# Moving steps between slots and engines in a split-fp32 macaron layer: the weights' transposes, the affinities, and five low parts of W_down

## The chip, the core and the metric

The kernel runs on one core of a Trainium2 chip. The metric is the device time of one execution, in microseconds. Its engines named here: TensorE (PE in the profile, with its weight loads as PEld), VectorE (DVE), ScalarE (ACT), GpSimd (POOL), SyncE (SP), which issues the transfers. Each works through its own instructions in the order in which they were written; semaphores hold an instruction until another engine's is done.

## What is computed

Eight sequences of 512 tokens and 128 features go through a feed-forward layer, an attention-like gate and the same feed-forward layer again.

```python
x = x + 0.5 * ffn(layernorm(x))
x = x + attn(layernorm(x))
x = x + 0.5 * ffn(layernorm(x))

# ffn, TOP_K = 8, 64 experts, each 128 -> 64 -> 128
shared = silu(xf @ Ws_up) @ Ws_down
aff = xf @ centroids.T
_, idx = top_k(aff + expert_biases, TOP_K)
w = sigmoid(take_along_axis(aff, idx, axis=1))
w = w / (sum(w) + 1e-8)
cw = zeros.at[tokens, idx].add(w)
h = silu(einsum('td,edf->etf', xf, W_up))
y = einsum('etf,efd->etd', h, W_down)
out = shared + einsum('etd,te->td', y, cw)

# attn: xf, xb are u times WB, WBf, with the first and the last row kept as they are
gamma = sigmoid(xf @ w1.T + xb @ w2.T + b)
y = gamma * (xf + xb) + (1 - gamma) * u
```

All experts are computed for all tokens; the routing enters as the weights cw, zero for an expert that was not chosen.

## The kernel before

**Phases and tiles.** One feed-forward layer of one sequence is a phase: 16 phases, numbered from 0. Even phases are a sequence's first layer, odd ones its second. Between the two lies the attention of that sequence, which is worked in the following phase beside other work. A phase has 33 tiles of 128 hidden features by 512 tokens: tile 0 is the shared expert, the others two features of each of the 64 experts. For each tile TensorE makes an up product into one of five PSUM banks (`up`), ScalarE applies silu, VectorE multiplies by `cw` (`gate`), ScalarE rounds to the high part `g_hi`, and VectorE (even tiles) or GpSimd (odd tiles) makes the low part `g_lo` by subtraction. A down product adds the tile into `y_ps`.

**Split products.** Each fp32 operand is split into a high and a low part, and a product is three matmuls, high by high, low by high, high by low (`split_product`, L697). The parts of W_up and W_down are made once, in phase 0, in eight pieces each: ScalarE makes the high parts (`wu_hi`, `wd_hi`), VectorE and GpSimd the low parts (`wu_lo`, `wd_lo`).

**Slots.** Every engine walks through a phase in 35 slots (`SLOTS`). In slot t TensorE does the down product of tile t-6 (`LAG`), then the up product of tile t. A down product waits for the low part of its tile (L755); an up product waits until the bank of tile t-5 is free, which for odd tiles is the gate's end and for even ones the low part's (`free_bank`, L766). Slots 0 to 5 still do down products of the phase before.

**Side steps.** What prepares the next phase or finishes the last is put between the tiles by tables, one for each kind of phase: a name and the slot after whose tile work the step stands. The same table is read by every engine. `AT_FIRST` is for phase 0, `AT_SECOND` for 1, `AT_THIRD` for 2, `AT_STEADY_A` and `AT_STEADY_B` for the loop's two phases (L119; it runs five times: phases 3 and 4, up to 11 and 12), and others for the last three. The steps that matter here, in their order:

- `x_t`, `x_hi`, `x_lo`: normalized tokens transposed by TensorE into `side1`, high part on ScalarE, low part on VectorE.
- `aff` (TensorE, L719, waits for x_lo), `aff_sum`, `bias`, `max`, `take` (VectorE), `sig` (ScalarE, which loads another activation table and then silu's again), `gate`, `sum`, `eps`, `inv` (VectorE), `cw` (GpSimd writes `w_dup`, L344), `cw_t` (TensorE transposes it into `side0`, L708), `cw_copy` (ScalarE, L404).
- `x1`, `stat1`, `aggr1`, `rstd1`, `norm1` (VectorE, with rstd on GpSimd), `xu` (GpSimd), `u_t` (TensorE, into `side1`), `u_copy` (ScalarE), `attn` (TensorE, L735, over both side banks, waits for u_copy and, in phases 2, 4, ..., 12, for cw_copy), `tanh` (ScalarE), `gamma` (GpSimd), `t1`, `x2` (VectorE), and again statistics and a normalization (`stat2` to `norm2`).

In phases 2, 4, ..., 12 all three chains run; in phase 0 the first two, and the splitting of the weights.

Of the kernel before, what the change touches and what calls it, by code (L numbers as in the profile page):

```python
# [17 lines left out]
LAG = RING + 1  # L18
# [18 lines left out]
class Phase:  # L37
# [19 lines left out]

NORM0 = ("stat0", "aggr0", "rstd0", "norm0")
AT_FIRST = {
    "x_t": 11, "x_hi": 12, "x_lo": 13, "aff": 15, "aff_sum": 15, "sig": 17, "bias": 16, "max": 17, "take": 17,  # L60
    "gate": 19, "sum": 21, "eps": 22, "inv": 24, "cw": 25, "cw_t": 33, "cw_copy": 33,
    "stat0": (1, 2), "aggr0": 3, "rstd0": 3, "norm0": (5, 6),
    "v": 11, "v_copy": 14, "wu_hi": (None, None, 2, 5, 8, 12, 15, 20),
    "wu_lo": (None, None, 3, 6, 9, 11, 17, 21), "wd_hi": (None, 4, 6, 12, 14, 19, 22, 26),
    "wd_lo": (None, 4, 8, 13, 16, 20, 24, 28),
    "late": 3,
}
AT_SECOND = {
# [6 lines left out]
    "y": 2, "keep": 26,  # L75
}
AT_THIRD = {
    "x_t": 4, "x_hi": 5, "x_lo": 5, "aff": 7, "aff_sum": 7, "sig": 9, "bias": 8, "max": 9, "take": 9,
    "gate": 11, "sum": 14, "eps": 15, "inv": 17, "cw": 18, "cw_t": 21, "cw_copy": 21,
    "y_t": 6, "x1": 8, "stat1": (10, 12), "aggr1": 13, "rstd1": 14, "norm1": (16, 18), "xu": 19, "u_t": 22,  # L80
    "u_copy": 22, "attn": 25, "tanh": 25, "gamma": 25, "t1": 25, "x2": (27, 28),
    "stat2": (29, 30), "aggr2": 30, "rstd2": 31, "norm2": (33, 34),
    "late": 3,
}
AT_STEADY_A = {
# [5 lines left out]
}  # L91
AT_STEADY_B = {
    "x_t": 1, "x_hi": 2, "x_lo": 4, "aff": 7, "aff_sum": 7, "sig": 9, "bias": 8, "max": 9, "take": 9,
    "gate": 11, "sum": 14, "eps": 15, "inv": 17, "cw": 18, "cw_t": 21, "cw_copy": 21,
    "y_t": 6, "x1": 8, "stat1": (10, 12), "aggr1": 13, "rstd1": 14, "norm1": (16, 18), "xu": 19, "u_t": 22,
    "u_copy": 22, "attn": 25, "tanh": 25, "gamma": 25, "t1": 25, "x2": (27, 28),
    "stat2": (29, 30), "aggr2": 30, "rstd2": 31, "norm2": (33, 34),
    "y": 2,
}
AT_MID_PREP = {  # L100
# [28 lines left out]
def build(nc, x, ident_in, cent_t, ebias, ws_up, ws_down, w_up, w_down, wb, wb_t, wbf, wbf_t, w1, w2, b_in, out):  # L129
    fp32, fp32r = mybir.dt.float32, mybir.dt.float32r  # L130
    ALU, ACT, AX = mybir.AluOpType, mybir.ActivationFunctionType, mybir.AxisListType
    ctx = ExitStack()
    with ctx:
        def sb(name, shape, dt=fp32):
            return ctx.enter_context(nc.sbuf_tensor(name, shape, dt))

        def sem(name):
            return ctx.enter_context(nc.semaphore(name))


# [39 lines left out]
        th, gamma = sb("th", [P, NB]), sb("gamma", [P, NB])  # L180
# [5 lines left out]
        aff = sb("aff", [P, NB, E])  # L186
        sig, biased, taken = sb("sig", [P, NB, E]), sb("biased", [P, NB, E]), sb("taken", [P, NB, E])
# [15 lines left out]
        consts_set, v_done, sm_hi_done, sm_lo_done = (sem(s) for s in ("consts_set", "v_done", "sm_hi_done", "sm_lo_done"))  # L203
        ce_hi_done, ce_lo_done = sem("ce_hi_done"), sem("ce_lo_done")
        v_copied, half_b_done = sem("v_copied"), sem("half_b_done")
        wu_hi_done, wd_hi_done, wd_lo_done = sem("wu_hi_done"), sem("wd_hi_done"), sem("wd_lo_done")
        wu_lo_done = [sem("wu_lo_done_vector"), sem("wu_lo_done_pool")]
        up_done, silu_done, gate_done, hi_done = (sem(s) for s in ("up_done", "silu_done", "gate_done", "hi_done"))
        lo_done = [sem("lo_done_vector"), sem("lo_done_pool")]
# [123 lines left out]
        @block.gpsimd  # L333
        def _(pool):
            def rstd_of(k, c):

                hold(pool, mv_done[k], c + 1)
                nc.gpsimd.tensor_scalar_add(var_eps[k][:, :], mv[k][:, :, 1], LN_EPS).then_inc(eps_done[k], 1)
                pool.wait_ge(eps_done[k], c + 1)
                nc.gpsimd.tensor_tensor(rstd[k][:, :], var_eps[k][:, :], neg_half[:, :], ALU.pow).then_inc(rstd_done[k], 1)  # L340

            def spread(q, n):
                pool.wait_ge(inv_done[q], n + 1)
                nc.gpsimd.tensor_tensor(*spread_operands, ALU.mult).then_inc(dup_done[q], 1)  # L344

            def low_part(ph, t):

                i = t % GRING
                pool.wait_ge(hi_done, NT * ph.p + t + 1)
                nc.gpsimd.tensor_tensor(g_lo[:, i, :], gated[:, t // 2 % ORING, :], g_hi[:, i, :].bitcast(fp32),  # L350
                                        ALU.subtract).then_inc(lo_done[1], 1)

            def split_up(i):

                js = slice(i * JS, (i + 1) * JS)
                pool.wait_ge(wu_hi_done, i + 1)
                nc.gpsimd.tensor_tensor(wu_lo[:, js, :], wu_raw[:, js, :], wu_hi[:, js, :].bitcast(fp32),
                                        ALU.subtract).then_inc(wu_lo_done[1], 1)

            def phase(ph):  # L360
                for t in range(SLOTS):
                    if (t - 1) % 2 and 0 < t <= NT:
                        low_part(ph, t - 1)
                    if t in ph.at.get("wu_lo", ()):
                        split_up(ph.at["wu_lo"].index(t))
                    for k, c in ((0, ph.norm0), (1, ph.mid), (2, ph.mid)):
                        if ph.at.get(f"rstd{k}") == t:
                            rstd_of(k, c)
                    if ph.at.get("xu") == t:
                        pool.wait_ge(norm_done[1], ph.mid + 1)  # L370
                        nc.gpsimd.tensor_tensor(xu[:, :, :], x1[:, :, :], normed[1][:, :, :], ALU.add).then_inc(xu_done, 1)
                    if ph.at.get("gamma") == t:

                        hold(pool, tanh_done, ph.mid + 1)
                        nc.gpsimd.tensor_scalar(gamma[:, :], th[:, :], 0.5, 0.5, ALU.mult, ALU.add).then_inc(gamma_done, 1)
                    if ph.at.get("keep") == t:

                        if ph.post is not None:
                            pool.wait_ge(out_done, ph.post + 1)
                        hold(pool, x2_done, ph.keep + 1)  # L380
# [12 lines left out]
        def _(act):
# [100 lines left out]
        def _(dve):  # L494
# [99 lines left out]
            def phase(ph):  # L594
                q = 1 - ph.q
                n = ph.prep[0] if ph.prep else None
                for t in range(SLOTS):
# [94 lines left out]
        def _(pe):  # L692
# [183 lines left out]
```

## Time and profile before

| | us |
|---|---|
| median of 3 runs | 828.2 (828.01 to 828.98) |
| profiled execution | 827.39 |
| its span | 825.6 |
| TensorE matmuls busy | 804.7 (97%) |
| VectorE busy | 690.8 (84%) |
| ScalarE busy | 653.8 (79%) |
| GpSimd busy | 402.9 (49%) |

The span is from the first to the last instruction of the profiled execution. Busy times of matmuls overlap: one 128x512 matmul is listed with about 0.40 us and the next starts 0.23 us after it. A row of a timeline gives start, duration, engine, source line, operation, output and inputs, and in brackets the idle time ahead of it with what ended it. Line numbers are those of the kernel before.

### The profile page before, as it was taken

How to read it: one execution, taken by the hardware profiler on the slowest of the kernel's cores; microseconds unless marked ns; L12 is line 12 of the kernel's file. 1: busy time of each engine (PE TensorE's matmuls, PEld its weight loads, DVE VectorE, ACT ScalarE, POOL GpSimd, SP SyncE). 2: the span in 40 equal slices, each digit the busy share in tenths (PEclk: the TensorE clock that was granted, in tenths of full speed). 3: DMA queues.
4: the chain of work that ended last, by engine and by line, in shares of the span. 5: the costliest groups of instructions: out<-in, count | busy, mean ns of one | idle time of the engine just before them, and what ended most of it. 6: DMA issues, size and time to landing. Idle time of an engine off the chain costs nothing.

```text
span 825.6 us, 12468 instructions
## 1 busy us (share of the span) xinstructions
PE 804.7 (97%) x3691; PEld 650.5 (79%) x3691; DVE 690.8 (84%) x1456; ACT 653.8 (79%) x1204; POOL 402.9 (49%) x355
## 2 busy tenths in 40 slices
PE   7899999999999999999999999999999999999998
PEld 5677877788887888878887888878888788888786
DVE  7898988888898887988879788797897978788875
ACT  5888678778797787877978778886888878876975
POOL 2654543545455454555535445353463644554443
PEclk9999999999999999999999999999999999999999
DMA  7000000000000000000000000000000000000000
GB/s 267 20 0 13 14 1 1 0 1 27 13 0 1 13 13 13 0 0 25 0 13 0 0 25 0 13 0 0 25 0 0 0 1 27 0 1 1 14 0 14
DMA packets 16046, 11.51 MB, mean 14 GB/s; under 512 B 1680, under 2 KB 14992, under 8 KB 16016
## 3 DMA queue, kind: packets, MB, share of 16 engines
q1 hardware_dynamic: 16016, 11.15, 4.3%
q8 instruction: 15, 0.25, 0.1%
q14 instruction: 15, 0.12, 0.1%
HBM read 9.05 MB, written 2.10 MB: 13 GB/s over the span
## 4 chain that ended last, share of the span: by engine, by line
PE 71%; DVE 16%; ACT 7%; issue 3%; POOL 3%; DMA 0%; DVEq 0%; ACTq 0%; POOLq 0%
PE up L700 11%; PE up L701 11%; PE up L699 11%; PE y_ps L699 11%; PE y_ps L701 10%; PE y_ps L700 10%; DVE up L568 3%; DVE gated L568 3%; PE side L708 3%; ACT g_hi L417 3%; DVE g_lo L577 2%; DVE normed L514 2%; ACT up L409 2%; POOL g_lo L350 1%; ACT L409 1%
## 5 line engine op out<-in xcount | busy, mean ns | idle before, releaser
L350 POOL TENSOR_TENSOR g_lo<-gated,g_hi 128x512 fp32r<-128x512 f32 x256 | 331.8, 1296 | 371.5 <-ACT g_hi L417 371.5
L409 ACT ACTIVATE up<-up 128x512 f32<-128x512 f32 x528 | 310.6, 589 | 82.1 <-PE up L701 80.0
L568 DVE TENSOR_TENSOR gated<-up,cw 128x512 f32<-128x512 f32 x256 | 175.2, 684 | 57.3 <-ACT up L409 53.3
L699 PE MATMUL y_ps<-g_hi,wd_hi 128*128 128x512 f32 x512 | 208.3, 407 | 1.8 <-POOL g_lo L350 1.7
L699 PE MATMUL up<-x_hi,wu_hi 128*128 128x512 f32 x512 | 202.6, 396 | 1.9 <-DVE g_lo L577 1.8
L701 PE MATMUL y_ps<-g_hi,wd_lo 128*128 128x512 f32 x512 | 202.6, 396 | 0.0
L700 PE MATMUL up<-x_lo,wu_hi 128*128 128x512 f32 x512 | 202.5, 396 | 0.0
L701 PE MATMUL up<-x_hi,wu_lo 128*128 128x512 f32 x512 | 201.7, 394 | 0.0
L700 PE MATMUL y_ps<-g_lo,wd_hi 128*128 128x512 f32 x512 | 201.5, 394 | 0.0
L568 DVE TENSOR_TENSOR up<-up,cw 128x512 f32<-128x512 f32 x256 | 176.3, 689 | 24.4 <-ACT up L409 21.4
L417 ACT CAST g_hi<-up 128x512 fp32r<-128x512 f32 x272 | 160.8, 591 | 36.8 <-DVE up L568 34.5
L577 DVE TENSOR_TENSOR g_lo<-up,g_hi 128x512 fp32r<-128x512 f32 x256 | 174.3, 681 | 10.6 <-ACT g_hi L417 9.3
L417 ACT CAST g_hi<-gated 128x512 fp32r<-128x512 f32 x256 | 157.3, 615 | 30.8 <-DVE gated L568 28.6
L699 PEld LDWEIGHTS up<-x_hi,wu_hi 128*128 128x128 f32 x512 | 96.3, 188 | 26.3 <-DVE g_lo L577 2.2
L699 PEld LDWEIGHTS y_ps<-g_hi,wd_hi 128*128 128x128 f32 x512 | 96.4, 188 | 25.4 <-POOL g_lo L350 3.7
L701 PEld LDWEIGHTS y_ps<-g_hi,wd_lo 128*128 128x128 f32 x512 | 96.2, 188 | 23.1
L700 PEld LDWEIGHTS up<-x_lo,wu_hi 128*128 128x128 f32 x512 | 96.3, 188 | 23.0
L701 PEld LDWEIGHTS up<-x_hi,wu_lo 128*128 128x128 f32 x512 | 96.3, 188 | 22.5
L700 PEld LDWEIGHTS y_ps<-g_lo,wd_hi 128*128 128x128 f32 x512 | 96.5, 189 | 18.8
L514 DVE TENSOR_SCALAR normed<-x,mv,rstd 128x128 f32<-128x128 f32 x64 | 35.1, 599 | 0.9 <-POOL rstd L340 0.9
L577 DVE TENSOR_TENSOR g_hi<-up,g_hi 64x512 fp32r<-64x512 f32 x16 | 11.1, 695 | 23.2 <-ACT g_hi L417 23.2
L340 POOL TENSOR_TENSOR rstd<-var_eps,neg_half 128x4 f32<-128x4 f32 x24 | 25.3, 1053 | 2.0
(100 smaller groups left out, 564.2 us busy)
## 6 DMA issues: line engine op xcount, KB each, us to landing
x_in<-in_x SPq DMA_DIRECT2D x8, 256.0 KB, 2.7
wu_raw<-in_w_up SPq DMA_DIRECT2D x4, 512.0 KB, 6.0
wd_raw<-in_w_down SPq DMA_DIRECT2D x4, 512.0 KB, 7.0
x_res<-in_x SPq DMA_DIRECT2D x8, 256.0 KB, 2.8
out<-out_sb SPq DMA_DIRECT2D x7, 256.0 KB, 2.2
out<-out_sb SPq DMA_DIRECT2D x2, 128.0 KB, 1.8
sm_raw<-in_ident SPq DMA_DIRECT2D x2, 64.0 KB, 5.4
ident<-in_ident SPq DMA_DIRECT2D x1, 64.0 KB, 2.3
```

The source lines that it names most:

```text
L340: nc.gpsimd.tensor_tensor(rstd[k][:, :], var_eps[k][:, :], neg_half[:, :], ALU.pow).then_inc(rstd_done[k], 1)
L350: nc.gpsimd.tensor_tensor(g_lo[:, i, :], gated[:, t // 2 % ORING, :], g_hi[:, i, :].bitcast(fp32), ALU.subtract).then_inc(lo_done[1], 1)
L409: nc.scalar.activation(up[i][:, :], up[i][:, :], ACT.Silu).then_inc(silu_done, 1)
L417: nc.scalar.copy(g_hi[:, t % GRING, :], src).then_inc(hi_done, 1)
L514: made = nc.vector.tensor_scalar(normed[k][:, n, :], norm_from[k][:, n, :], mv[k][:, n, 0:1], rstd[k][:, n:n + 1], ALU.subtract, ALU.mult)
L568: nc.vector.tensor_tensor(gated[:, t // 2 % ORING, :] if t % 2 else up[i][:, :], up[i][:, :], cw[ph.q][:, :], ALU.mult).then_inc(gate_done, 1)
L577: nc.vector.tensor_tensor(lo[ps, i, :], up[t % RING][ps, :], g_hi[ps, i, :].bitcast(fp32), ALU.subtract).then_inc(lo_done[0], 1)
L699: nc.tensor.matmul(o, a[0], b[0], start=start, stop=False)
L700: nc.tensor.matmul(o, a[0], b[1], start=False, stop=False)
L701: return nc.tensor.matmul(o, a[1], b[0], start=False, stop=stop)
L708: last = nc.tensor.transpose(rows(dst, n), src(n), ident[:, :])
```

## The change

It moves entries of three tables and gives part of one step to another engine.

- In `AT_THIRD` and `AT_STEADY_B` (phases 2, 4, ..., 12) `cw_t` and `cw_copy` go from slot 21 to 23, `attn`, `tanh`, `gamma`, `t1` from 25 to 26, `x2`, `stat2`, `aggr2`, `rstd2` one slot back.
- In `AT_THIRD` (phase 2 only) `aff` and `aff_sum` go from 7 to 9, `bias`, `sig`, `max`, `take`, `gate` two slots back, `sum` and `eps` one.
- In `AT_FIRST` (phase 0) `x_lo` goes from 13 to 12, `aff` and what follows it up to `eps` one slot back.
- Of the eight pieces of `wd_lo`, VectorE makes the first three as before, GpSimd the other five, in slots 13, 15, 20, 23 and 27 (they were in 13, 16, 20, 24 and 28 on VectorE). TensorE waits for GpSimd's pieces on a semaphore of their own.

```diff
+VW = 3
@@ AT_FIRST
-    "x_t": 11, "x_hi": 12, "x_lo": 13, "aff": 15, "aff_sum": 15, "sig": 17, "bias": 16, "max": 17, "take": 17,
-    "gate": 19, "sum": 21, "eps": 22, "inv": 24, "cw": 25, "cw_t": 33, "cw_copy": 33,
+    "x_t": 11, "x_hi": 12, "x_lo": 12, "aff": 16, "aff_sum": 16, "sig": 18, "bias": 17, "max": 18, "take": 18,
+    "gate": 20, "sum": 22, "eps": 23, "inv": 24, "cw": 25, "cw_t": 33, "cw_copy": 33,
...
-    "wd_lo": (None, 4, 8, 13, 16, 20, 24, 28),
+    "wd_lo": (None, 4, 8, 13, 15, 20, 23, 27),
@@ AT_THIRD
-    "x_t": 4, "x_hi": 5, "x_lo": 5, "aff": 7, "aff_sum": 7, "sig": 9, "bias": 8, "max": 9, "take": 9,
-    "gate": 11, "sum": 14, "eps": 15, "inv": 17, "cw": 18, "cw_t": 21, "cw_copy": 21,
+    "x_t": 4, "x_hi": 5, "x_lo": 5, "aff": 9, "aff_sum": 9, "sig": 11, "bias": 10, "max": 11, "take": 11,
+    "gate": 13, "sum": 15, "eps": 16, "inv": 17, "cw": 18, "cw_t": 23, "cw_copy": 23,
...
-    "u_copy": 22, "attn": 25, "tanh": 25, "gamma": 25, "t1": 25, "x2": (27, 28),
-    "stat2": (29, 30), "aggr2": 30, "rstd2": 31, "norm2": (33, 34),
+    "u_copy": 22, "attn": 26, "tanh": 26, "gamma": 26, "t1": 26, "x2": (28, 29),
+    "stat2": (30, 31), "aggr2": 31, "rstd2": 32, "norm2": (33, 34),
@@ AT_STEADY_B: cw_t, cw_copy, attn to rstd2 as in AT_THIRD
...
@@ GpSimd
+            def split_down(i):
+                js = slice(i * JS, (i + 1) * JS)
+                pool.wait_ge(wd_hi_done, i + 1)
+                nc.gpsimd.tensor_tensor(wd_lo[:, js, :], wd_raw[:, js, :], wd_hi[:, js, :].bitcast(fp32),
+                                        ALU.subtract).then_inc(wd_lo_done[1], 1)
...
                     if t in ph.at.get("wu_lo", ()):
                         split_up(ph.at["wu_lo"].index(t))
+                    if t in ph.at.get("wd_lo", ())[VW:]:
+                        split_down(ph.at["wd_lo"].index(t))
@@ VectorE
-                    if t in ph.at.get("wd_lo", ()):
+                    if t in ph.at.get("wd_lo", ())[:VW]:
@@ TensorE
-                        pe.wait_ge(wd_lo_done, (t - LAG - 1) // JS + 1)
+                        i = (t - LAG - 1) // JS
+                        pe.wait_ge(wd_lo_done[i >= VW], i + 1 - VW * (i >= VW))
```

TensorE's queue in phase 2 around slots 21 and 22, before. `w_dup` are the spread weights, `normed1` the tokens for the attention; a product is three rows:

```order
L701 MATMUL up1<-x_hi0,wu_lo 128x512
L708 MATMUL side<-ident,w_dup 128x128 x4
L699 MATMUL y_ps<-g_hi,wd_hi 128x512
L700 MATMUL y_ps<-g_lo,wd_hi 128x512
L701 MATMUL y_ps<-g_hi,wd_lo 128x512
L699 MATMUL up2<-x_hi0,wu_hi 128x512
L700 MATMUL up2<-x_lo0,wu_hi 128x512
L701 MATMUL up2<-x_hi0,wu_lo 128x512
L708 MATMUL side<-ident,normed1 128x128 x4
L699 MATMUL y_ps<-g_hi,wd_hi 128x512
```

The same place after the change, slots 22 and 23. The line numbers are those of the changed file:

```order
L713 MATMUL up2<-x_hi0,wu_lo 128x512
L720 MATMUL side<-ident,normed1 128x128 x4
L711 MATMUL y_ps<-g_hi,wd_hi 128x512
L712 MATMUL y_ps<-g_lo,wd_hi 128x512
L713 MATMUL y_ps<-g_hi,wd_lo 128x512
L711 MATMUL up3<-x_hi0,wu_hi 128x512
L712 MATMUL up3<-x_lo0,wu_hi 128x512
L713 MATMUL up3<-x_hi0,wu_lo 128x512
L720 MATMUL side<-ident,w_dup 128x128 x4
L711 MATMUL y_ps<-g_hi,wd_hi 128x512
```

The weights' transposes stood ahead of the u transposes, at the end of slot 21; they now stand behind them, at the end of slot 23, two down and two up products later. Phases 4 to 12 have the same order.

GpSimd's queue in phase 0 from slot 11, before. `g_lo` are low parts of odd tiles, `wu_lo` and `wd_lo` pieces of the weights' low parts:

```order
L357 TENSOR_TENSOR wu_lo<-wu_raw,wu_hi 128x512
L350 TENSOR_TENSOR g_lo<-gated,g_hi 128x512 x3
L357 TENSOR_TENSOR wu_lo<-wu_raw,wu_hi 128x512
L350 TENSOR_TENSOR g_lo<-gated,g_hi 128x512 x2
L357 TENSOR_TENSOR wu_lo<-wu_raw,wu_hi 128x512
L350 TENSOR_TENSOR g_lo<-gated,g_hi 128x512 x2
L344 TENSOR_TENSOR w_dup<-w_sel,w_inv 128x512
L350 TENSOR_TENSOR g_lo<-gated,g_hi 128x512 x8
```

And after the change:

```order
L360 TENSOR_TENSOR wu_lo<-wu_raw,wu_hi 128x512
L353 TENSOR_TENSOR g_lo<-gated,g_hi 128x512
L367 TENSOR_TENSOR wd_lo<-wd_raw,wd_hi 128x512
L353 TENSOR_TENSOR g_lo<-gated,g_hi 128x512
L367 TENSOR_TENSOR wd_lo<-wd_raw,wd_hi 128x512
L353 TENSOR_TENSOR g_lo<-gated,g_hi 128x512
L360 TENSOR_TENSOR wu_lo<-wu_raw,wu_hi 128x512
L353 TENSOR_TENSOR g_lo<-gated,g_hi 128x512 x2
L367 TENSOR_TENSOR wd_lo<-wd_raw,wd_hi 128x512
L360 TENSOR_TENSOR wu_lo<-wu_raw,wu_hi 128x512
L353 TENSOR_TENSOR g_lo<-gated,g_hi 128x512
L367 TENSOR_TENSOR wd_lo<-wd_raw,wd_hi 128x512
```

Five pieces of `wd_lo` have come between the low parts (the fifth stands four rows further on). Around slots 20 to 22 two pieces stand between the low parts of tiles 19 and 21.

VectorE's queue in phase 0 from slot 12, before. `gated<-up3` is the gate of tile 13, `up2<-up2` that of tile 12:

```order
L568 TENSOR_TENSOR up2<-up2,cw0 128x512
L568 TENSOR_TENSOR gated<-up3,cw0 128x512
L577 TENSOR_TENSOR g_lo<-up2,g_hi 128x512
L583 TENSOR_TENSOR wd_lo<-wd_raw,wd_hi 128x512
L521 TENSOR_TENSOR x_lo1<-side,x_hi1 128x512
L568 TENSOR_TENSOR up4<-up4,cw0 128x512
L609 TENSOR_SCALAR b_half<-b_col 128x1
L611 COPY sm_raw<-side 128x2
L612 COPY sm_raw<-side 128x2
L568 TENSOR_TENSOR gated<-up0,cw0 128x512
```

And after the change:

```order
L580 TENSOR_TENSOR up2<-up2,cw0 128x512
L533 TENSOR_TENSOR x_lo1<-side,x_hi1 128x512
L580 TENSOR_TENSOR gated<-up3,cw0 128x512
L589 TENSOR_TENSOR g_lo<-up2,g_hi 128x512
L580 TENSOR_TENSOR up4<-up4,cw0 128x512
L621 TENSOR_SCALAR b_half<-b_col 128x1
L623 COPY sm_raw<-side 128x2
L624 COPY sm_raw<-side 128x2
L580 TENSOR_TENSOR gated<-up0,cw0 128x512
L589 TENSOR_TENSOR g_lo<-up4,g_hi 128x512
```

`x_lo1`, for which the affinities wait, has gone ahead of tile 13's gate and low part, and `wd_lo` is gone from between.

## Rows read from the trace of the kernel before

**Rows 1.** Page, busy us of each engine, share of the span, instructions.

```profile
PE 804.7 (97%) x3691; PEld 650.5 (79%) x3691; DVE 690.8 (84%) x1456; ACT 653.8 (79%) x1204; POOL 402.9 (49%) x355
```

**Rows 2.** Waits of TensorE: us in total, times, longest.

```profile
PE side L708 <- POOL w_dup L344: 5.9, 7, 0.9
PE side L719 <- DVE x_lo L521: 4.1, 3, 2.6
...
PE up L699 <- DVE g_lo L577: 1.8, 3, 0.9
```

**Rows 3.** TensorE timeline, phase 4, slots 21 to 23; last row 100 us on (start, us, instruction, [idle]).

```profile
251.24 0.39 PE L701 MATMUL up<-x_hi,wu_lo 128*128 128x512 f32 x1
252.55 0.66 PE L708 MATMUL side<-ident,w_dup 128*128 128x128 f32 x4 [0.92 <-POOL w_dup L344]
252.96 0.48 PE L699 MATMUL y_ps<-g_hi,wd_hi 128*128 128x512 f32 x1
...
253.75 0.39 PE L699 MATMUL up<-x_hi,wu_hi 128*128 128x512 f32 x1
...
254.45 0.60 PE L708 MATMUL side<-ident,normed 128*128 128x128 f32 x4
254.80 0.47 PE L699 MATMUL y_ps<-g_hi,wd_hi 128*128 128x512 f32 x1
...
255.58 0.39 PE L699 MATMUL up<-x_hi,wu_hi 128*128 128x512 f32 x1
...
352.44 0.66 PE L708 MATMUL side<-ident,w_dup 128*128 128x128 f32 x4 [0.86 <-POOL w_dup L344]
```

**Rows 4.** VectorE timeline, phase 4: second half of the normalization, low part of tile 18.

```profile
250.66 1.92 DVE L514 TENSOR_SCALAR normed<-x,mv,rstd 128x128 f32<-128x128 f32 x2
...
253.10 0.67 DVE L577 TENSOR_TENSOR g_lo<-up,g_hi 128x512 fp32r<-128x512 f32 x1
```

**Rows 5.** GpSimd timeline, phase 4: spread weights.

```profile
251.46 1.04 POOL L344 TENSOR_TENSOR w_dup<-w_sel,w_inv 128x512 f32<-128x512 f32 x1
```

**Rows 6.** ScalarE timeline, phase 4: high part in slot 23.

```profile
257.49 0.63 ACT L417 CAST g_hi<-up 128x512 fp32r<-128x512 f32 x1
```

**Rows 7.** TensorE timeline, phase 4: start of attention.

```profile
259.07 0.38 PE L740 MATMUL side<-sm_raw,u_mid 128*128 128x130 f32 x2
```

**Rows 8.** TensorE timeline, phase 2: last up matmul of slot 7, affinities, next product.

```profile
129.72 0.40 PE L701 MATMUL up<-x_hi,wu_lo 128*128 128x512 f32 x1
...
131.07 0.33 PE L719 MATMUL side<-ce_both,x_hi 128*128 128x128 f32 x1 [0.96 <-DVE x_lo L521]
...
131.99 0.48 PE L699 MATMUL y_ps<-g_hi,wd_hi 128*128 128x512 f32 x1
```

**Rows 9.** VectorE timeline, phase 2: second half of the normalization.

```profile
150.77 1.92 DVE L514 TENSOR_SCALAR normed<-x,mv,rstd 128x128 f32<-128x128 f32 x2
```

**Rows 10.** TensorE timeline, phase 0: slot 15, affinities, down product 21, phase 1's start.

```profile
35.09 0.40 PE L701 MATMUL up<-x_hi,wu_lo 128*128 128x512 f32 x1
38.05 0.33 PE L719 MATMUL side<-ce_both,x_hi 128*128 128x128 f32 x1 [2.55 <-DVE x_lo L521]
...
55.91 0.39 PE L699 MATMUL y_ps<-g_hi,wd_hi 128*128 128x512 f32 x1
...
67.47 0.39 PE L699 MATMUL up<-x_hi,sm_hi 128*128 128x512 f32 x1
```

**Rows 11.** VectorE's wd_lo from 30 to 66 us: duration ns min/median/max.

```profile
L583 DVE TENSOR_TENSOR wd_lo<-wd_raw,wd_hi x6: 680/1539/1810, 28.6 to 62.4; 128x512 fp32r<-128x512 f32 x6
```

**Rows 12.** VectorE timeline, phase 0: gate of tile 13 and the idle time before it.

```profile
35.51 0.69 DVE L568 TENSOR_TENSOR gated<-up,cw 128x512 f32<-128x512 f32 x1 [1.73 <-ACT up L409]
```

**Rows 13.** GpSimd, groups from 36 to 66 us: busy, mean ns, idle before.

```profile
L350 POOL TENSOR_TENSOR g_lo<-gated,g_hi 128x512 fp32r<-128x512 f32 x10 | 13.1, 1306 | 13.1 <-ACT g_hi L417 13.1
L357 POOL TENSOR_TENSOR wu_lo<-wu_raw,wu_hi 128x512 fp32r<-128x512 f32 x2 | 3.5, 1736 | 0.0
```

**Rows 14.** GpSimd timeline, phase 0: low part of tile 19.

```profile
50.55 1.30 POOL L350 TENSOR_TENSOR g_lo<-gated,g_hi 128x512 fp32r<-128x512 f32 x1 [1.91 <-ACT g_hi L417]
```

More of the change, by code:

```diff
@@ L93 @@
     "x_t": 1, "x_hi": 2, "x_lo": 4, "aff": 7, "aff_sum": 7, "sig": 9, "bias": 8, "max": 9, "take": 9,
-    "gate": 11, "sum": 14, "eps": 15, "inv": 17, "cw": 18, "cw_t": 21, "cw_copy": 21,
+    "gate": 11, "sum": 14, "eps": 15, "inv": 17, "cw": 18, "cw_t": 23, "cw_copy": 23,
     "y_t": 6, "x1": 8, "stat1": (10, 12), "aggr1": 13, "rstd1": 14, "norm1": (16, 18), "xu": 19, "u_t": 22,
-    "u_copy": 22, "attn": 25, "tanh": 25, "gamma": 25, "t1": 25, "x2": (27, 28),
-    "stat2": (29, 30), "aggr2": 30, "rstd2": 31, "norm2": (33, 34),
+    "u_copy": 22, "attn": 26, "tanh": 26, "gamma": 26, "t1": 26, "x2": (28, 29),
+    "stat2": (30, 31), "aggr2": 31, "rstd2": 32, "norm2": (33, 34),
     "y": 2,
@@ L205, in build @@
         v_copied, half_b_done = sem("v_copied"), sem("half_b_done")
-        wu_hi_done, wd_hi_done, wd_lo_done = sem("wu_hi_done"), sem("wd_hi_done"), sem("wd_lo_done")
+        wu_hi_done, wd_hi_done = sem("wu_hi_done"), sem("wd_hi_done")
+        wd_lo_done = [sem("wd_lo_done_vector"), sem("wd_lo_done_pool")]
         wu_lo_done = [sem("wu_lo_done_vector"), sem("wu_lo_done_pool")]
@@ L604, in phase @@
                         low_part(ph, t - 1)
-                    if t in ph.at.get("wd_lo", ()):
-                        split_low(wd_lo, wd_raw, wd_hi, ph.at["wd_lo"].index(t), wd_hi_done, wd_lo_done)
+                    if t in ph.at.get("wd_lo", ())[:VW]:
+                        split_low(wd_lo, wd_raw, wd_hi, ph.at["wd_lo"].index(t), wd_hi_done, wd_lo_done[0])
                     if ph.at.get("v_copy") == t:
@@ L680, in _ @@
             nc.vector.tensor_tensor(*spread_operands, ALU.mult).then_inc(first_dup_done, 1)
-            split_low(wd_lo, wd_raw, wd_hi, 0, wd_hi_done, wd_lo_done)
+            split_low(wd_lo, wd_raw, wd_hi, 0, wd_hi_done, wd_lo_done[0])
             over_phases(dve, phase)
```

## The prediction

> **What bounds the kernel now.** I read the page's busy table first, then the waits of TensorE, then its timeline around each wait, then the timelines of the engines it waits for. TensorE is busy 97% of the span [rows 1], but matmuls overlap, so that share doesn't say what a wait costs. The timeline does: a product of three 128x512 matmuls takes 0.70 us (253.75 to 254.45), 0.23 a matmul, and they follow each other without a gap nearly everywhere [rows 3]. So the kernel's time is the TensorE queue plus its waits, and other engines matter only where they make TensorE wait. The waits that bear on this change are three kinds [rows 2]: the transposes of the weights wait for GpSimd's w_dup (5.9 us, 7 times), the affinities wait for x_lo (4.1, 3 times), up products wait for VectorE's g_lo (1.8, 3 times). I count a wait as the distance of two starts less what it is without one, since the listed idle leaves out some pipeline refill.
>
> A slot t is one tile: down product of tile t-6, up product of tile t. An up product needs the bank of tile t-5, a down product the low part of tile t-6.
>
> **Part 1: transposes from slot 21 to 23, attention from 25 to 26 (phases 2, 4, 6, 8, 10, 12).** In phase 4 the last up matmul of slot 21 starts at 251.24 and the transposes at 252.55, 1.31 later; unwaited it is 0.23. That is 1.08. The waited group then holds the queue 0.41 (to 252.96), the unwaited one at 254.45 holds it 0.35 (to 254.80): 0.06 more. So 1.14 a phase [rows 3]. The six waits look alike; the seventh of the row is phase 15's, which is not edited.
> What comes late instead? Without the wait slot 22 starts at 251.47, its up product at 252.17, and the u transposes at 252.87. They need VectorE's norm, whose second half ends at 250.66+1.92 = 252.58: 0.29 to spare. The next up product follows 1.13 behind a turn (254.45 to 255.58), so at 254.00; it needs the bank of tile 18, freed at 253.10+0.67 = 253.77: 0.23 to spare [rows 3, 4]. Neither VectorE nor ScalarE is paced by TensorE there, so these ends stand still while TensorE moves up. The moved transposes come at 254.70; w_dup ended at 251.46+1.04 = 252.50 [rows 5]. On ScalarE the copy of the weights goes behind the high part that stands at 257.49, so it ends by 258.7 even with nothing gained in front of it [rows 6]. Attention stood 4.62 behind the u transposes (254.45 to 259.07); add the weights' turn (0.43) and one slot (1.40), and it comes at 252.87+6.45 = 259.32, 0.6 behind that copy [rows 3, 7]. Queued behind attention are the down and up products of slot 27 on TensorE, and tanh and the next silu on ScalarE, as before. The x2 and statistics steps move one slot with it; VectorE then has half of the second statistics and the aggregates behind tile 30's low part rather than ahead of it, so the banks at the phase's change get more room, and the last normalization less. I take all of this as hidden. Value 5 x 1.14 = 5.7 for the loop's phases. Bounds: 0.29 and 0.23 are thin; if the VectorE chain takes back half it is 2.9, and above 5.7 there is nothing to win.
>
> **Part 2: affinities of phase 2, slot 7 to 9, with their chain.** The affinities start 1.35 behind the last up matmul (129.72 to 131.07) instead of 0.23: 1.12 [rows 8]. Two slots later x_lo has long been done. With part 1 that would be 2.26. But phase 2's norm ends at 150.77+1.92 = 152.69 [rows 9], and TensorE, 2.26 and the moved turn's 0.43 earlier than before, would be at its u transposes at 151.87. The VectorE chain wins perhaps 0.3 there, because sigmoid's two table loads start later and nearer to a caught-up queue, so about 0.5 comes back as a new wait. Value 1.8. Bounds: 0.9 (the chain stands still and slot 9 crowds it) and 2.3.
>
> **Part 3: phase 0.** x_lo goes from slot 13 to 12 on VectorE, affinities from 15 to 16 on TensorE; five of VectorE's wd_lo go to GpSimd, in slots 13, 15, 20, 23, 27. From the last up matmul of slot 15 at 35.09 to the affinities at 38.05 it takes 2.96 instead of 0.23 [rows 10]. From the end of slot 15's up product (35.32) to phase 1's first product (67.47) are 32.15 us. In them stand 37 products (20 down, 17 up) of 0.70, 25.9; the affinities, 0.92 from 131.07 to 131.99 [rows 8]; the weights' turn, 0.43: 27.25. So no more than 4.9 can go.
> VectorE sheds five wd_lo, median 1.54, maximum 1.81 [rows 11], some 7 us, most of what made it late. Behind tile 12's gate it idles 1.73 until 35.51, for ScalarE [rows 12]; x_lo at slot 12 falls nearly into that hole and ends near 35.7, ahead of the affinities, which would come near 36.7.
> GpSimd gains 5 x 1.3 to 1.74 = 6.5 to 8.7 us; from 36 to 66 it idles 13.1 [rows 13]. That idle is not where the pieces stand: in slots 20 to 22 its queue is g_lo(19), wd_lo, wu_lo, g_lo(21). TensorE's new waits on GpSimd's wd_lo are at slots 19, 23, 27 and 31, with a down and an up product queued behind each; I find each piece there at least a slot early, so it is g_lo behind the piece that is late. g_lo(19) began at 50.55 [rows 14]. With sigmoid a slot later and VectorE rid of two pieces I put it at 47.8. Then 1.30+1.30+1.45+1.30 gives g_lo(21) at 53.15, where TensorE wants it at 52.1: a new wait of 1.0. Down product 21 stood at 55.91 [rows 10], so TensorE is 2.8 ahead there. From it to 67.47 are 11.56 us, of which 15 products and a turn fill 10.93; those 0.6 of small waits go too: 3.4. For what I have not seen I take 3.2. Bounds: with g_lo(19) 1.0 later and each split 1.74, 1.4; at worst 0.8; at best 4.9.
>
> A rule beside this. The trace has wd_lo on VectorE at 1.54 median against 0.68 for its shortest [rows 11], and GpSimd's wu_lo at 1.74 against 1.31 for g_lo [rows 13]. The Trainium skill's "SBUF — State Buffer", section "Who interferes with whom", says a VectorE instruction with two SBUF inputs and a GpSimd one that reads SBUF exclude each other for the whole instruction. By it the pieces on GpSimd would run at 1.3, as their partners on VectorE are gone, and the biased sums on VectorE would collide more often. By the rule part 3 gives 3.4, by the wu_lo row for every piece 2.6.
>
> **Sum.** 5.7 + 1.8 + 3.2 = 10.7. The profiled execution took 827.39 (span 825.6 and 1.8 around it); it becomes 816.7. The runs' median, 828.2, lies 0.8 above it: 817.5.
>
> **Rivals.**
> - VectorE's chain takes back part of the turn's wait: at the u transposes or at up product 23. For: 0.29 and 0.23 to spare. Against: both are positive with nothing slower. Half of five waits back, 2.9: 820.4.
> - GpSimd bounds phase 0: split, split and low part in a row, each up to 1.74. For: slots 20 to 23. Against: 13.1 us of idle time [rows 13]. Phase 0 gives 1.0: 819.7.
> - No new wait anywhere, phase 0 at its floor: 5.7+2.3+4.9 = 12.9: 815.3.
> - The first two together: 822.6.
> - On the other side: GpSimd's queue in phase 0. Each piece stands before a low part, and each low part holds a down product; if TensorE has caught up with that queue, each piece lands on it whole, 5 x 1.74 = 8.7, with nothing saved in phase 0. It decides once the 13.1 idle lie where no piece stands. Then 7.5 won and 8.7 lost: 829.4. Against: only slots 20 to 23 are tight.
>
> **How the numbers follow.** Forecast 0.60 (its own range 816.0 to 819.0), VectorE's chain 0.14, GpSimd bound 0.12, no new wait 0.07, both 0.04, the slower side 0.03. The range goes from the floor, 815.2, to between the last two, 821.3. Under 0.2% (1.7 us) nothing can be told from no change. Faster by more: 0.95; within: 0.02; slower: 0.03.
>
> **What would show it.** In the profile after: w_dup among TensorE's waits once only, 0.7; one loop iteration (turn to turn, 252.55 to 352.44 before [rows 3]) 98.75 us instead of 99.9; no wait before the affinities but phase 0's start; a wait near down product 21 of phase 0 on GpSimd's g_lo, and phase 1's first up product near 64.2. Wrong would be: a wait at the u transposes in each loop phase, a wait of attention for the weights' copy, or a third or more of phase 0's gain lost behind wd_lo.

## The result, and the profile after

The changed kernel takes 821.76 us (median of 4 runs, 821.68 to 821.94), the one before 828.11 (4 runs, 827.44 to 828.98): a ratio of 0.9923, 95% interval 0.9906 to 0.994, a gain of 6.35 us. The forecast was 817.5 with a range of 815.2 to 821.3. The sign was right, the size was not: 10.7 us were forecast, and the time lies 0.46 outside the range. The profiled execution shows a span of 820.0, where 814.9 was forecast (816.7 less the 1.8 around it).

The page, busy time of each engine; it answers to [rows 1]:

```profile
PE 805.1 (98%) x3691; PEld 649.5 (79%) x3691; DVE 692.7 (84%) x1451; ACT 650.7 (79%) x1204; POOL 408.3 (50%) x360
```

GpSimd has five instructions more and VectorE five fewer. Yet VectorE is busy 1.9 us longer, although five pieces of some 1.5 us have left it. Something on VectorE has become slower. The waits of TensorE, after; they answer to [rows 2]:

```profile
PE up L711 <- DVE g_lo L589: 3.4, 10, 0.6
PE side L720 <- DVE normed L526: 2.0, 3, 1.3
...
PE side L720 <- POOL w_dup L347: 0.6, 1, 0.6
...
PE side L731 <- DVE x_lo L533: 0.6, 1, 0.6
```

What the change aimed at is gone: w_dup is waited for once instead of seven times, x_lo once, at the kernel's start. New is the first row: up products wait for VectorE's low part ten times (3.4 us) instead of three (1.8). Six of the ten stand at one place, the first product of phases 3, 5, ..., 13. TensorE's timeline there, after, phase 5's start (start, us, instruction, idle ahead):

```profile
267.86 0.40 PE L713 MATMUL y_ps<-g_hi,wd_lo 128*128 128x512 f32 x1
268.49 0.50 PE L711 MATMUL up<-x_hi,sm_hi 128*128 128x512 f32 x1 [0.23 <-DVE g_lo L589]
268.83 0.40 PE L712 MATMUL up<-x_lo,sm_hi 128*128 128x512 f32 x1
```

Unwaited, the product would start at 268.09. It starts 0.40 late (0.40 to 0.52 at the six places), and its second matmul 0.34 behind it instead of 0.23. Six slots on, the phase's first down product (behind an up matmul at 274.71) loses 0.16 and the refill again. It waits for ScalarE's copy of y_ps, which ends at 275.05 (ScalarE, then TensorE):

```profile
274.47 0.58 ACT L434 COPY y_sb<-y_ps 128x512 f32<-128x512 f32 x1
```

```profile
275.10 0.50 PE L774 MATMUL y_ps<-g_hi,sm_hi 128*128 128x512 f32 x1
```

That copy stands in ScalarE's queue behind a high part (273.94) whose gate VectorE made late (273.21), so it goes back to the same lateness of VectorE.

Each phase, from one first up product to the next, in us (phases 3 and 4 stand for the loop's five iterations):

| phase | before | after | gained | forecast |
|---|---|---|---|---|
| 0 | 56.86 | 53.71 | 3.15 | 3.2 |
| 1 | 51.02 | 50.97 | 0.05 | 0 |
| 2 | 54.83 | 53.43 | 1.40 | 1.8 |
| 3 | 48.05 | 48.50 | -0.45 | 0 |
| 4 | 51.84 | 51.17 | 0.67 | 1.14 |
| 3 to 12 together | 499.28 | 498.04 | 1.24 | 5.7 |

(499.28 is 173.32 to 672.60, 498.04 is 168.82 to 666.86.) The shortfall is in the loop: 4.5 of the 5.1 us that the span misses. Phase 2 lacks 0.4 and phase 13, which follows the same kind of phase, 0.3.

**Where the loop's gain went.** The edited places did what they should. TensorE's timeline, after, phase 4, slots 22 and 23 and attention; it answers to [rows 3, 7]:

```profile
248.66 0.40 PE L713 MATMUL up<-x_hi,wu_lo 128*128 128x512 f32 x1
248.90 0.60 PE L720 MATMUL side<-ident,normed 128*128 128x128 f32 x4
249.25 0.48 PE L711 MATMUL y_ps<-g_hi,wd_hi 128*128 128x512 f32 x1
...
250.74 0.60 PE L720 MATMUL side<-ident,w_dup 128*128 128x128 f32 x4
...
255.13 0.39 PE L713 MATMUL up<-x_hi,wu_lo 128*128 128x512 f32 x1
255.36 0.38 PE L752 MATMUL side<-sm_raw,u_mid 128*128 128x130 f32 x2
```

Both groups of transposes follow the matmul ahead of them by 0.24, attention by 0.23: no wait at any. Attention stands 6.46 behind the u transposes, where 6.45 was forecast. What comes after it does not hold. VectorE's timeline, before, phase 4, the two halves of x2:

```profile
266.12 0.60 DVE L644 SCALAR_TENSOR_TENSOR x<-t,gamma,xu 128x128 f32<-128x128 f32 x2
266.65 0.69 DVE L568 TENSOR_TENSOR up<-up,cw 128x512 f32<-128x512 f32 x1
267.25 1.35 DVE L644 SCALAR_TENSOR_TENSOR x<-t,gamma,xu 128x128 f32<-128x128 f32 x2
```

And after:

```profile
261.82 1.67 DVE L656 SCALAR_TENSOR_TENSOR x<-t,gamma,xu 128x128 f32<-128x128 f32 x2
...
264.61 1.65 DVE L656 SCALAR_TENSOR_TENSOR x<-t,gamma,xu 128x128 f32<-128x128 f32 x2
266.18 0.69 DVE L580 TENSOR_TENSOR up<-up,cw 128x512 f32<-128x512 f32 x1
...
267.76 0.67 DVE L589 TENSOR_TENSOR g_lo<-up,g_hi 128x512 fp32r<-128x512 f32 x1
```

GpSimd's timeline, after, beside them:

```profile
261.78 1.29 POOL L353 TENSOR_TENSOR g_lo<-gated,g_hi 128x512 fp32r<-128x512 f32 x1 [3.02 <-ACT g_hi L429]
264.82 1.29 POOL L353 TENSOR_TENSOR g_lo<-gated,g_hi 128x512 fp32r<-128x512 f32 x1 [1.74 <-ACT g_hi L429]
```

A half of x2 (two instructions) takes 0.60 by itself and 1.35 to 1.67 beside one of GpSimd's low parts. Before, one half of the two met one; one slot later both do. From there the chain is this: x2's second half ends late, so the gate of tile 30 (the row at 266.18) is late. ScalarE idles for it:

```profile
266.90 0.59 ACT L429 CAST g_hi<-up 128x512 fp32r<-128x512 f32 x1 [1.52 <-DVE up L580]
```

The low part of tile 30 ends at 268.43, and the next phase's first product, which wants its bank, starts at 268.49. All instructions of x2, before and then after (busy, mean ns):

```profile
L644 DVE SCALAR_TENSOR_TENSOR x<-t,gamma,xu 128x128 f32<-128x128 f32 x32 | 16.0, 546 | 0.0
```

```profile
L656 DVE SCALAR_TENSOR_TENSOR x<-t,gamma,xu 128x128 f32<-128x128 f32 x32 | 24.3, 802 | 0.0
```

That is 8.3 us more on VectorE; it outweighs the five pieces that are gone (10.2 us of wd_lo before, 2.8 after); with 1.1 more for `w_sel`, see below, it makes about the 1.9 of the page. The Trainium skill's "SBUF — State Buffer", section "Who interferes with whom", has the rule that fits: a VectorE instruction with two SBUF inputs and a GpSimd one that reads SBUF shut each other out for a whole instruction. Here x2 reads t and xu. This trace agrees: the held half at 261.82 ends at 263.49, 0.42 behind the end of the low part. The prediction cited this rule for wd_lo and did not apply it to x2.

**Phase 0.** TensorE's timeline, after, phase 0 at slot 15 and phase 1's start; it answers to [rows 10]:

```profile
35.25 0.40 PE L713 MATMUL up<-x_hi,wu_lo 128*128 128x512 f32 x1
35.49 0.40 PE L711 MATMUL y_ps<-g_hi,wd_hi 128*128 128x512 f32 x1
...
64.42 0.39 PE L711 MATMUL up<-x_hi,sm_hi 128*128 128x512 f32 x1
```

There is no wait at slot 15 or before the affinities, and phase 1's first product stands at 64.42 (forecast near 64.2). GpSimd's queue in slots 19 to 21, after; it answers to [rows 14]:

```profile
48.01 1.30 POOL L353 TENSOR_TENSOR g_lo<-gated,g_hi 128x512 fp32r<-128x512 f32 x1 [3.54 <-ACT g_hi L429]
49.28 1.47 POOL L367 TENSOR_TENSOR wd_lo<-wd_raw,wd_hi 128x512 fp32r<-128x512 f32 x1
50.71 1.29 POOL L360 TENSOR_TENSOR wu_lo<-wu_raw,wu_hi 128x512 fp32r<-128x512 f32 x1
51.96 1.30 POOL L353 TENSOR_TENSOR g_lo<-gated,g_hi 128x512 fp32r<-128x512 f32 x1
```

Forecast were 47.8 for the first start and 53.15 for the last one as the moment at which it is done; it is done at 53.26. But TensorE had lost 0.45 at up product 23 and 0.77 at 25 already, so down product 21 waited 0.28 only, instead of 1.0. The waits at up products 23 and 25 are for VectorE's low parts, with different causes. Up product 25 goes back to the weights' selection, which takes 1.55 beside GpSimd's low part at 48.01 (0.42 elsewhere):

```profile
48.04 1.55 DVE L561 SCALAR_TENSOR_TENSOR w_sel<-taken,sig 128x256 f32<-128x256 f32 x1
```

Up product 23 waits for the low part of tile 18, which stands on VectorE behind the gate of tile 19; that gate (45.93, idle 0.59 before it) waits for the silu that ScalarE does behind the sigmoid and its two table loads:

```profile
42.29 1.28 ACT L412 ACT_TABLE_LOAD   x1
...
44.02 1.28 ACT L421 ACT_TABLE_LOAD   x1
```

### The profile page after: what moved, and what is told of

Same layout as the page of the kernel before. It is cut to its first block, busy times and chain, and to the rows that moved or that the text cites. A ratio compares the mean times of both kernels' runs of the same rounds, so it can differ in the third digit from the quotient of the medians.

```text
span 820.0 us, 12468 instructions
## 1 busy us (share of the span) xinstructions
PE 805.1 (98%) x3691; PEld 649.5 (79%) x3691; DVE 692.7 (84%) x1451; ACT 650.7 (79%) x1204; POOL 408.3 (50%) x360
## 4 chain that ended last, share of the span: by engine, by line
PE 77%; DVE 14%; ACT 5%; issue 1%; POOL 1%; DMA 0%; DVEq 0%; ACTq 0%; POOLq 0%
PE up L711 12%; PE up L712 12%; PE up L713 12%; PE y_ps L711 11%; PE y_ps L713 11%; PE y_ps L712 11%; PE side L720 3%; DVE x L656 3%; DVE g_lo L589 2%; DVE gated L580 2%; ACT up L421 2%; ACT g_hi L429 2%; DVE normed L526 2%; DVE up L580 2%; PE side L731 1%
## 5 line engine op out<-in xcount | busy, mean ns | idle before, releaser
L429 ACT CAST g_hi<-up 128x512 fp32r<-128x512 f32 x272 | 161.2, 592 | 47.8 <-DVE up L580 45.8
```

Of the source, the lines that this page charges most:

```text
L429: nc.scalar.copy(g_hi[:, t % GRING, :], src).then_inc(hi_done, 1)
```

## The experiments

Their names: x2_back, t1_psum, turn_only, t1_psum_before, pieces_vector, aff_chain_old, x2_back_psum, best_try. The first four were timed beside 19 runs of the kernel before (median 829.19, 827.42 to 829.99), the last four beside 8 (829.22, 827.47 to 829.99).

### x2_back: the changed kernel, x2 and the statistics in their old slots

```diff
-    ... "t1": 26, "x2": (28, 29), "stat2": (30, 31), "aggr2": 31, "rstd2": 32,
+    ... "t1": 26, "x2": (27, 28), "stat2": (29, 30), "aggr2": 30, "rstd2": 31,
```

> The changed kernel with x2, stat2, aggr2 and rstd2 of phases 2, 4, ..., 12 at the slots they had before (27/28, 29/30, 30, 31), attention staying at 26. Theory A (port): the move put both halves of x2, which reads two SBUF tensors, beside a GpSimd low part (1.67 and 1.65 us instead of 0.60 and 1.35). Moved back, the first half takes about 0.6 again, tile 30's low part is early enough, and the two new waits at the phase change (0.40 to 0.43 before up product 0, 0.15 before down product 0, and their refill) go: a loop iteration 98.8 us instead of 99.6, in all about 817. Theory B (room): x2 half 1 now follows attention by one slot less, VectorE has the same work at the phase's end and the waits stay or move: 821 to 822. Theory C: TensorE's 1.14 earlier arrival alone makes the waits; moving back helps by half: 819.

Measured: 816.83 us (816.51 to 816.9), ratio 0.9856 (0.984 to 0.9873). Phases 2, 3 and 4 take 53.03, 48.01 and 50.68; phases 3 to 12 together 493.82, a gain of 5.46 where 5.7 was forecast, and phase 2 gains 1.80, where 1.8 was. VectorE's two halves of x2, phase 4, and GpSimd beside them:

```profile
259.94 0.61 DVE L656 SCALAR_TENSOR_TENSOR x<-t,gamma,xu 128x128 f32<-128x128 f32 x2
...
261.06 1.34 DVE L656 SCALAR_TENSOR_TENSOR x<-t,gamma,xu 128x128 f32<-128x128 f32 x2
```

```profile
260.70 1.29 POOL L353 TENSOR_TENSOR g_lo<-gated,g_hi 128x512 fp32r<-128x512 f32 x1 [2.96 <-ACT g_hi L429]
```

The first half ends at 260.55, just ahead of the low part; only the second is held. No wait is left at the phase's change, although TensorE comes there earlier than in the changed kernel, so theory C falls with theory B. This alone does not separate two causes, since x2 is both a slot earlier and unheld.

### t1_psum: the changed kernel, its slots kept, t1 in PSUM

```diff
-  nc.vector.tensor_tensor(t1[:, :, :], att[:, :, 0:D], normed[1][:, :, :], ...
+  nc.vector.tensor_tensor(att[:, :, 0:D], att[:, :, 0:D], normed[1][:, :, :], ...
-  nc.vector.scalar_tensor_tensor(x2[:, m, :], t1[:, m, :], gamma[:, m:m + 1], xu[:, m, :], ...
+  nc.vector.scalar_tensor_tensor(x2[:, m, :], att[:, m, 0:D], gamma[:, m:m + 1], xu[:, m, :], ...
```

> The changed kernel with t1 left in the attention's PSUM banks, so that x2 reads one SBUF tensor instead of two; every slot stays. Theory A (port): both halves of x2 fall from about 1.66 to 0.55 us, no wait at the phase change, about 817. Theory B (the slots are too late, whatever the duration): x2 shorter or not, the waits at the phase change stay, 821 to 822.

Measured: 815.27 us (815.06 to 815.68), ratio 0.984 (0.9823 to 0.9856). VectorE and GpSimd, phase 4, slots as in the changed kernel:

```profile
259.96 0.60 DVE L656 SCALAR_TENSOR_TENSOR x<-side,gamma,xu 128x128 f32<-128x128 f32 x2
...
261.95 0.60 DVE L656 SCALAR_TENSOR_TENSOR x<-side,gamma,xu 128x128 f32<-128x128 f32 x2
```

```profile
259.92 1.29 POOL L353 TENSOR_TENSOR g_lo<-gated,g_hi 128x512 fp32r<-128x512 f32 x1 [2.96 <-ACT g_hi L429]
```

And all 32 instructions of x2:

```profile
L656 DVE SCALAR_TENSOR_TENSOR x<-side,gamma,xu 128x128 f32<-128x128 f32 x32 | 9.5, 343 | 0.0
```

The first half lies wholly beside GpSimd's low part and takes 0.60 all the same; what changed is that one of its inputs is in PSUM, in the attention's own banks. The waits at the phase's change are gone although nothing moved, and the loop takes 493.82, as in x2_back. So it was x2 being held up by GpSimd, and not the slot. The 1.6 us below x2_back come mostly from phases 1 (50.37 instead of 50.98), 2 (52.66 instead of 53.03) and 14 (50.37 instead of 50.69), where x2 was held too.

### turn_only: the kernel before, with the turn, attention and x2 moved in phases 2, 4, ..., 12

```diff
-    "cw_t": 21, "cw_copy": 21, ... "attn": 25, ... "x2": (27, 28), ...
+    "cw_t": 23, "cw_copy": 23, ... "attn": 26, ... "x2": (28, 29), ...
```

> The kernel before with part 1 alone: weights' transposes at 23, attention at 26 and what follows it, in phases 2, 4, ..., 12; phase 0 and phase 2's affinities as before. If the parts add up and the changed kernel's traces are read rightly, each loop iteration gains 0.3 net (1.14 less 0.84 at the phase change) and phase 2 about the same: 1.8 to 2 in all, 826.2. If part 1 were worth what was forecast (1.14 each) and the shortfall came from the other parts, 821.3.

Measured: 827.21 us (825.7 to 828.39, 10 runs), ratio 0.9981 (0.997 to 0.9992). An iteration takes 99.5 (48.42 and 51.1) against 99.9; x2 has a mean of 804 ns. Against the runs beside it that is 2.0 us less, where 1.8 to 2 was expected. The waits at the first products of phases 3, 5, ..., 13 are there. So the small gain of the loop and its new waits come from this part alone, not from the moved affinities or from GpSimd's pieces.

### t1_psum_before: the kernel before with t1 in PSUM

The edit is that of t1_psum.

> The kernel before with t1 in PSUM alone, a control: x2 falls from 0.60 and 1.35 to 0.55 each, but nobody waits at the phase change there, so both theories expect no change, 828.1 within 0.3.

Measured: 827.56 us (826.05 to 828.53, 10 runs), ratio 0.9983 (0.9973 to 0.9993). No change was expected; 1.6 us came, and at the full clock (see the last section) 1.4 to 1.8, 826.05 against 827.4 to 827.9. It comes from phases 1, 2 and 14 (0.80, 0.41 and 0.37), not from the loop. There an iteration still takes 99.9: no product of the loop waited for x2, and the waits for w_dup stay (0.82 to 0.90). The same edit gives some 6.5 us on top of the change and 1.6 without it.

### pieces_vector: the changed kernel, all eight pieces of wd_lo on VectorE

```diff
-VW = 3
+VW = 8
-    "wd_lo": (None, 4, 8, 13, 15, 20, 23, 27),
+    "wd_lo": (None, 4, 8, 13, 16, 20, 24, 28),
```

> The changed kernel, but VectorE makes all eight pieces of wd_lo again (slots 13, 16, 20, 24, 28); x_lo at slot 12 and the affinities at 16 stay. Changed kernel: 821.76, phase 0 53.71. Theory X (the 3.2 us of phase 0 come from x_lo's move alone: it falls into a hole of VectorE, and TensorE's 2.7 us wait goes): phase 0 within 0.8 of 53.7, 821.5 to 822.5, although VectorE carries 7 us more. Theory P (x_lo's move only shifts the wait; VectorE is late all through slots 13 to 28, and the pieces' going is what lets the gain through): the pieces at about 1.5 us each make g_lo late for up products, phase 0 55.5 to 57, 823.5 to 825. In both the wait before the affinities stays away, and with it the slow matmuls behind it.

Measured: 826.34 us (825.42 to 827.25, 5 runs), ratio 0.997 (0.9956 to 0.9984); phase 0 takes 57.38, more than before (56.86). TensorE in it:

```profile
46.80 0.40 PE L713 MATMUL y_ps<-g_hi,wd_lo 128*128 128x512 f32 x1
49.07 0.50 PE L711 MATMUL up<-x_hi,wu_hi 128*128 128x512 f32 x1 [1.87 <-DVE g_lo L589]
...
50.26 0.63 PE L712 MATMUL y_ps<-g_lo,wd_hi 128*128 128x512 f32 x1
50.69 0.63 PE L713 MATMUL y_ps<-g_hi,wd_lo 128*128 128x512 f32 x1
```

The wait before the affinities is gone, but up product 23 waits 2.04 instead of 0.45: x_lo's move by itself only shifts the wait. Behind it eight matmuls come 0.43 apart instead of 0.23, some 1.5 us more, which neither theory expected. With them phase 0 and the median lie above what theory P gave (57 and 825). Without them phase 0 would be 55.9 or somewhat more, an estimate inside theory P's range: TensorE, that much earlier, might wait longer at up product 25. Theory X, at 53.7 give or take 0.8, falls either way.

### aff_chain_old: the changed kernel, phase 0's affinities in their old slots

```diff
-    "x_lo": 12, "aff": 16, "aff_sum": 16, "sig": 18, "bias": 17, "max": 18, "take": 18, "gate": 20, ...
+    "x_lo": 13, "aff": 15, "aff_sum": 15, "sig": 17, "bias": 16, "max": 17, "take": 17, "gate": 19, ...
```

> The changed kernel, but in phase 0 x_lo, the affinities and what follows them stand in the slots of the kernel before (13, 15, ...); GpSimd keeps its five pieces of wd_lo. Theory X (x_lo's move carries the gain): x_lo stands behind gate and low part of tile 13 and 12 again, so TensorE waits about 2.1 us before the affinities (2.7 less the 0.6 of the piece that is gone); some of it is absorbed by the 1.5 us of later waits; phase 0 54.5 to 56, median 822.5 to 824.5. Theory P (the pieces carry it): phase 0 within 0.5 of 53.7. On the clock: if the idle stretch before the affinities is what sometimes lowers TensorE's granted clock, the runs of this kernel spread over 1.5 us or more again; if it comes from something else, they spread over 0.3 to 0.6 as the other kernels without the wait.

Measured: 823.19 us (822.73 to 824.97, 4 runs), ratio 0.9933 (0.9916 to 0.995); phase 0 takes 55.09. The wait before the affinities is there:

```profile
35.29 0.40 PE L713 MATMUL up<-x_hi,wu_lo 128*128 128x512 f32 x1
37.66 0.33 PE L731 MATMUL side<-ce_both,x_hi 128*128 128x128 f32 x1 [1.97 <-DVE x_lo L533]
```

It is 2.14, as expected, and swallows the later ones at up products 23 and 25; down product 21 waits 0.64 for GpSimd. This run came out as theory X had it, the last one nearer to theory P. Of phase 0's 3.15 us the pieces alone give 1.77 (56.86 to 55.09), and the moved chain on top of them 1.38 (55.09 to 53.71). Alone, the chain costs 0.5 as measured (pieces_vector); by the estimate without the slow matmuls it would give 1.0 at most. So neither theory had it whole: the pieces carry more than half, and the chain's part came only with them.

### x2_back_psum: both remedies

The edits of x2_back and t1_psum together.

> The changed kernel with both remedies: x2 and the statistics in the slots of the kernel before (27, 28) and t1 in PSUM. Alone they gave 816.83 and 815.27. If both only take away the same late x2 (port theory), they don't add: 815.0 to 815.5, loop iteration 98.7. If the slots cost something of their own beside it, 813.5 to 814.5.

Measured: 815.21 us (815.05 to 815.31), ratio 0.9832 (0.9815 to 0.9848), no different from t1_psum's 815.27. The two remedies do not add: both take away the same late x2.

### best_try: the two remedies, and phase 0 smoothed

```diff
-    "gate": 20, "sum": 22, ...
+    "gate": 19, "sum": 22, ...
-    "wd_lo": (None, 4, 8, 13, 15, 20, 23, 27),
+    "wd_lo": (None, 4, 8, 13, 15, 22, 24, 27),
```

> As x2_back_psum, and in phase 0 the weights' selection goes from slot 20 to 19 (ahead of tile 20's gate, so before GpSimd's low part of tile 19, beside which it took 1.55 us) and GpSimd's sixth and seventh piece of wd_lo from 20 and 23 to 22 and 24 (behind the low part of tile 21, instead of ahead of it). Phase 0's waits at up 23 (0.45), up 25 (0.77) and down 21 (0.28) should go, 1.5 us: 813.7 to 814.2 with 815.2 for x2_back_psum. If sigmoid isn't ready at slot 19, VectorE waits there and the gain is 0.5 or less, or turns into a loss.

Measured: 815.11 us (814.92 to 815.16), ratio 0.983 (0.9813 to 0.9846): the same as x2_back_psum. VectorE's selection and TensorE at down product 21:

```profile
47.13 0.42 DVE L561 SCALAR_TENSOR_TENSOR w_sel<-taken,sig 128x256 f32<-128x256 f32 x1
```

```profile
53.14 0.50 PE L711 MATMUL y_ps<-g_hi,wd_hi 128*128 128x512 f32 x1 [0.40 <-POOL wd_lo L367]
```

The selection takes 0.42 instead of 1.55 once it is out of the way of GpSimd's low part, and up product 25 waits 0.24 instead of 0.77. But down product 21 needs the very piece that was moved behind: it waits 0.57 for it. Up product 23 waits 0.45 as before, so that wait was not the selection's. Of the 1.5 us expected 0.35 came (53.79 to 53.44). By these waits the selection's part was worth having and the pieces' part not; they were not run apart. This median is the lowest of all, 6.65 us below the changed kernel, but t1_psum is within 0.2 of it with two lines.

## Why the prediction was wrong

- **The failed step** is in part 1: "The x2 and statistics steps move one slot with it; ... so the banks at the phase's change get more room ... I take all of this as hidden." The banks got less room. The statistics did go behind tile 30's low part, but each half of x2 came to lie beside a low part of GpSimd, 1.37 us more a phase on VectorE (1.67 and 1.65 against 0.60 and 1.35). Out of it came waits of 0.40 to 0.52 at the next phase's first up product and of 0.16 at its first down product, and the refills behind them. Five iterations gave 1.24 instead of 5.7. x2_back and t1_psum show it from two sides.
- **Part 1's other steps held.** No wait at the u transposes, at the moved turn or at attention; with x2 unheld the loop gives 5.46, against 5.7. The thin margins of 0.29 and 0.23 were enough, so the rival in which VectorE's chain takes back half at the u transposes or at up product 23 was wrong in place, and too small (2.9 back, 4.5 measured). A wait at the phase's change had no chance in the list at all.
- **Part 2** came to 1.40 instead of 1.8: its new wait at the u transposes was 0.40 (about 0.5 forecast), and the missing 0.4 is x2 again (1.80 in x2_back).
- **Part 3** was right in size, 3.15 for 3.2, and the forecast start and end of GpSimd's queue were within 0.25. Its one wait of 1.0 was three, of 0.45, 0.77 and 0.28, in all 1.5. Only the last is GpSimd's. The 0.45 goes back to ScalarE's sigmoid, the 0.77 to the w_sel that takes 1.55 beside GpSimd's low part (best_try takes away most of the second and none of the first). That the size came out all the same is in part luck. The rival in which GpSimd bounds phase 0 did not occur.
- **From the profile to the runs**: 0.8 us was added because before's median lay above its profiled execution. That was a property of the kernel before (below), and fell away with the change: the changed kernel's median lies 1.8 above its span, as the execution alone would have it. Without that term the forecast would have been 816.7, 5.1 too low, which is the 4.5 of the loop, 0.4 of phase 2 and 0.3 of phase 13.

## What to carry to other kernels

When a step is moved by a slot, list what every other engine does beside its new place, not only who waits for it: two VectorE instructions that read two SBUF tensors each cost 0.60 us together in one slot and 1.67 in the next, where a GpSimd instruction lies. With one of the two inputs in PSUM they took 0.60 beside it as well, so their price did not depend on the slot; that was worth 6.5 us here and 1.6 before, where the loop's phases did not wait for them. And where a margin after the edit is counted in tenths, the last steps of the phase need to be walked through like the first.

## What the runs showed of the hardware

**The clock behind a wait.** The kernel before and each that keeps a wait of over 2 us in phase 0 spread over 1.8 to 2.7 us from run to run; the others over 0.2 to 0.6. The records say why. Windows of the turn_only execution (stretch, its length, busy time of PE, PEld, DVE, ACT and POOL, then the granted clock as a share of the full one: 1.00, 0.52, 0.62, 1.00):

```profile
37.00:39.00 2.00, 0.77 (x7) 0.77 (x7) 2.00 (x7) 1.38 (x4) 1.44 (x1) 1.00 0.00 0
39.00:41.00 2.00, 2.00 (x8) 1.67 (x7) 1.76 (x3) 0.92 (x2) 0.00 (x0) 0.52 0.00 0
41.00:43.00 2.00, 2.00 (x7) 1.56 (x6) 0.24 (x1) 0.85 (x2) 0.00 (x0) 0.62 0.00 0
43.00:45.00 2.00, 2.00 (x11) 1.61 (x10) 2.00 (x2) 1.45 (x4) 1.67 (x2) 1.00 0.00 0
```

And TensorE in it:

```profile
38.23 0.33 PE L719 MATMUL side<-ce_both,x_hi 128*128 128x128 f32 x1 [2.57 <-DVE x_lo L521]
...
40.20 0.63 PE L701 MATMUL y_ps<-g_hi,wd_lo 128*128 128x512 f32 x1
40.63 0.63 PE L699 MATMUL up<-x_hi,wu_hi 128*128 128x512 f32 x1
```

TensorE had stood idle 2.57 us, worked for about a microsecond, and then ran at half its clock (1.2 instead of 2.4 GHz) from 39.1 to 42.5: 0.43 us a matmul, 1.5 us in all. In t1_psum_before the half clock lasts from 38.0 to 44.7, so it is there as soon as TensorE starts again, and phase 0 takes 59.17; in pieces_vector it follows the 2.04 us wait at up product 23, from 49.9 to 53.3. In the profiled execution of before it did not occur (1.00 throughout, 56.86). The runs of before show it by their mean clock: at 1.000 they took 827.4 to 827.9, at 0.997 and 0.998 828.2 to 829.3, at 0.995 829.7 to 830.0. So part 3 also took away a chance of losing up to 2.5 us, which no row of the one profiled execution shows; compared at the full clock, the change gave 5.7 to 6.1 us. In aff_chain_old, with a wait of 2.14, one run of four had it (0.998, 824.97 against 822.7 to 823.2); none of the 20 runs of the five kernels without such a wait had it (mean clock 0.999 to 1.000). What decides in which run it comes is not shown.

**GpSimd's side of a meeting with VectorE.** The two wu_lo of [rows 13] took 1.74 and 1.73 us, each beside a wd_lo of 1.80 and 1.81 on VectorE. In the changed kernel, where VectorE makes none there, they take 1.32 and 1.29, as g_lo does; the five wd_lo on GpSimd take 1.30 to 1.47. So both engines pay for such a meeting.
